# Two Gaussian blurs with a width per pixel: the exponents made on TensorE, the quotients turned on VectorE

## What is computed

```python
h = relu(einsum('bchw,co->bohw', x, w1) + b1[None, :, None, None])          # 32 hidden channels
ks = relu(einsum('bohw,o->bhw', h, w2[:, 0]) + b2[0]) * 20.0 + 1.0          # a width per pixel
sigma = ks / 3.0
logits = -gauss_kernel[None, None, None] / (2.0 * sigma[..., None, None] ** 2)
wgt = exp(logits)                                                            # 9 x 9 per pixel
wgt = wgt / sum(wgt, axis=(-2, -1), keepdims=True)
low_freq = sum over (u, v) of xp[:, :, u:u+64, v:v+64] * wgt[..., u, v]      # xp: x padded by 4
enhanced = x + low_freq
out = (enhanced - mean) / sqrt(var + 1e-5)                                   # over the plane
```

## Time and profile before

| | us |
|---|---|
| median of three runs | 515.1 |
| the three runs | 514.4, 515.1, 520.95 |
| span of the profiled execution, first to last instruction | 516.5 |
| TensorE busy in it | 431.7 (84%) |
| VectorE busy | 374.6 (73%) |
| ScalarE busy | 279.2 (54%) |
| GpSimd busy | 57.2 (11%) |

### The profile page before, as it was taken

One profiled execution on the slowest core, in us unless ns is written; L12 is line 12 of the kernel. 1 busy time (PEld: TensorE's weight loads), 2 busy tenths in 40 slices (PEclk: granted clock), 3 DMA queues, 4 the chain that ended last, 5 costly groups with the idle time before them and its releaser, 6 DMA issues. The chain is left out here.

```text
span 516.5 us, 16761 instructions
## 1 busy us (share of the span) xinstructions
PE 431.7 (84%) x7248; PEld 311.4 (60%) x7248; DVE 374.6 (73%) x563; ACT 279.2 (54%) x382; POOL 57.2 (11%) x76
## 2 busy tenths in 40 slices
PE   4578998877999649689999998469978899999971
PEld 2277952224988512357777787357746687777860
DVE  2695486763888875488999999239525899999953
ACT  0655476663333200189888888211015888888753
POOL 3230002321000000310000120000030000000000
PEclk9968999997999959999999999869987999999986
DMA  8840000000000000000000000000000000000004
GB/s 189 173 171 1 2 1 0 1 0 1 3 3 1 3 0 0 0 2 4 3 4 1 0 2 4 3 1 1 0 0 1 3 4 3 3 0 1 3 4 162
DMA packets 8088, 9.79 MB, mean 19 GB/s; under 512 B 5391, under 2 KB 6752, under 8 KB 7904
## 3 DMA queue, kind: packets, MB, share of 16 engines
q1 hardware_dynamic: 7008, 8.60, 6.0%
q10 hardware_dynamic: 1024, 0.36, 0.4%
HBM read 6.85 MB, written 2.11 MB: 17 GB/s over the span
## 5 line engine op out<-in xcount | busy, mean ns | idle before, releaser
L1110 DVE TENSOR_TENSOR g_wgt<-g_exponents,ps 128x1024 f32<-128x1024 f32 x128 | 150.9, 1206 | 4.4 <-PE ps L955 4.3
L1054 ACT ACTIVATE g_wgt<-g_wgt 128x1024 f32<-128x1024 f32 x128 | 132.4, 1061 | 18.6 <-DVE g_wgt L1110 17.7
L955 PE MATMUL ps<-ident,g_scl 128*128 128x128 f32 x512 | 78.9, 283 | 4.5 <-DVE g_scl L1101 3.6
L970 PE MATMUL ps<-g_wgt,g_xt 128*32 128x64 f32 x4096 | 72.6, 223 | 7.5 <-issue 7.4
L970 PEld LDWEIGHTS ps<-g_wgt,g_xt 128*32 128x32 f32 x4096 | 62.0, 111 | 27.2 <-issue 24.1
L955 PEld LDWEIGHTS ps<-ident,g_scl 128*128 128x128 f32 x512 | 56.3, 139 | 16.0 <-DVE g_scl L1101 4.7
L1038 ACT ACTIVATE g_hid<-ps,vec 128x512 f32<-128x512 f32 x32 | 22.0, 688 | 64.5 <-PE ps L914 64.5
L469 PE MATMUL ps<-conv_img,projblk 128*32 128x512 f32 x256 | 35.4, 673 | 0.0
L1351 PE MATMUL ps<-high,wb 128*128 128x512 f32 x72 | 30.6, 426 | 5.3 <-DVE rest L1380 5.3
L526 ACT ACTIVATE biased<-ps,beta_o 128x512 f32<-128x512 f32 x32 | 23.5, 746 | 13.6 <-PE ps L469 13.5
L1061 ACT COPY g_num<-ps 128x512 f32<-128x512 f32 x32 | 18.5, 578 | 22.0 <-PE ps L970 22.0
(11 more groups left out here) (163 smaller groups left out, 688.8 us busy)
## 6 DMA issues: line engine op xcount, KB each, us to landing
x<-in_x SPq DMA_DIRECT2D x8, 256.0 KB, 6.9
x<-in_x SPq DMA_DIRECT2D x1, 2048.0 KB, 8.2
out<-g_result SPq DMA_DIRECT2D x4, 512.0 KB, 3.9
windows<-band SPq DMA_DIRECT2D x4, 256.0 KB, 4.9
c_weight<-in_c_weight SPq DMA_DIRECT2D x1, 576.0 KB, 3.8
g_w<-in_g_w SPq DMA_DIRECT2D x2, 128.0 KB, 2.6
onehot<-in_onehot ACTq DMA_DIRECT2D x1, 128.0 KB
g_gband<-in_g_gband SPq DMA_DIRECT2D x2, 64.0 KB, 2.8
```

The source lines that it names most:

```text
L955: tr = pe.transpose(ps[:, u % 4, P * k:P * k + P], spread(scl[s][:, k, u:u + 1], [P, P]), ident[:])
L970: mm = pe.matmul(ps[32 * j:32 * j + 32, O_BANK, 64 * cb:64 * cb + 64], xt[(s + t) % 2][:, cb, b, :], wgt[s][b][:, t, cb, :], start=(t == 0 ...
L1054: act.activation(w, w, ACT.Exp).then_inc(weight, 1)
L1110: dve.tensor_tensor(wgt[s][u][:], spread(gband[:].unsqueeze(2), shape), spread(s_in, shape), ALU.mult).then_inc(logit, 1)
```

## The change

**Exponents.** The widths of a row no longer go through spreading and a product. GpSimd makes diagonal blocks (`pool_diag`): 32 x 32 matrices with the scale of a pixel on the diagonal, 16 of them side by side in 512 columns. TensorE multiplies the constant exponents, now stationary with pixels first, with these (`pe_fill`): four matmuls with K=32, one on each 32 partitions, into four PSUM banks. One call fills the exponents of two exponentials; a blur has 32 calls. ScalarE's exponential (`act_weight`) reads two banks of PSUM, 1,024 columns, and writes `wgt`. Three pairs of banks take turns.

**Quotients.** VectorE turns the numerators straight out of PSUM in blocks of 32 x 32 (`dve_swing`), divides (`dve_mix`) and turns the result back (`dve_low`); GpSimd adds it to the image (`pool_enhance`). TensorE and ScalarE have no part in this any more.

**Widths and turned image first.** The hidden layer of all eight rows stands at the start, its matmul as two with K=64, its relu half on ScalarE and half on VectorE; the scales come in two batches of four rows. All nine row groups of the image are turned before the fourth fill. The staged image lies in `wgt` buffers that aren't yet in use. The loop over rows is gone.

The core of the diff; the functions that it takes away are those printed above.

```diff
-        for name, shape in (("gmask", [P, 2, BLK * BLK]), ("outblk", [P, 2, 64]),
+        for name, shape in (("gmask", [P, 2, P]), ("outblk", [P, 2, 64]), ("hot", [P, 32]),
...
-    tile = [sb(f"tile{s}", [P, CB, BLK, QC]) for s in range(2)]
+    gband = sb("exponents", [P, 2, P])
+    hid = [[sb(f"hid{s}{i}", [P, CB, BLK, BLK]) for i in range(2)] for s in range(2)]
+    relu = sb("relu", [P, BANK])
+    sm = [sb(f"sm{i}", [P, 4 * 4 * B]) for i in range(2)]
+    scl = [sb(f"scl{i}", [P, 4, 4 * B]) for i in range(2)]
+    diag = [[sb(f"diag{s}{h}", [P, 16, 32]) for h in range(2)] for s in range(2)]
+    MX = C + 1
+    xt = [sb(f"xt{g}", [P, CB, B, MX]) for g in range(RB + 1)]
...
+    KS_BANK, XT_BANK, O_BANK = (4, 5), (6, 7), (6, 7)
+    BATCH = 4
+    XT_ON_ACT = 3
...
+        return 2 * (n % 3)
+    def pe_hidden(pe, r):
+        if r >= 2:
+            for i in range(2):
+                pe.wait_ge(hid_out[i], r - 1)
+        for i in range(2):
+            part = slice(64 * i, 64 * i + 64)
+            pe.matmul(ps[:, 2 * (r % 2) + i, :], w1[part, i, :],
+                      pad[part, BLK * r + R:BLK * r + R + BLK, R:R + W], start=True, stop=True).then_inc(hid_mm, 1)
...
+    def act_hidden(act, r):
+        act.wait_ge(hid_mm, 2 * r + 1)
+        if r >= 2:
+            act.wait_ge(ks_mm, r - 1)
+        act.activation(hid_to(r, 0), hid_in(r, 0), ACT.Relu, bias=vec[:, VEC[tag + "_b1"]:VEC[tag + "_b1"] + 1],
+                       scale=1.0).then_inc(hid_out[0], 1)
+    def dve_hidden(dve, r):
+        dve.wait_ge(hid_mm, 2 * r + 2)
+        if r >= 2:
+            dve.wait_ge(ks_mm, r - 1)
+        dve.tensor_scalar(hid_to(r, 1), hid_in(r, 1), vec[:, VEC[tag + "_b1"]:VEC[tag + "_b1"] + 1], 0.0,
+                          ALU.add, ALU.max).then_inc(hid_out[1], 1)
...
+    def tile(g):
+        spare = wgt[1][g // 4 % 2][:].rearrange("p t v u a n -> p (t v u a n)")
+        return spare[:, 1024 * (g % 4):1024 * (g % 4) + 1024].rearrange("p (k r c) -> p k r c", k=CB, r=BLK)
...
+    def pe_xt(pe, g):
+        pe.wait_ge(staged, 2 * g + 2)
+        for k in range(2):
+            if g > 0:
+                xt_evacuated(pe, g - 1, k)
+            for j in range(4):
+                cb = 4 * k + j
+                tr = pe.transpose(ps[:, XT_BANK[k], P * j:P * j + P],
+                                  tile(g)[:, cb].rearrange("p r c -> p (r c)"), ident[:])
+            tr.then_inc(xt_mm, 1)
+    def xt_copy(eng, copy, g, k, done):
+        eng.wait_ge(xt_mm, 2 * g + k + 1)
+        copy(xt[g][:, 4 * k:4 * k + 4, :, 0:C],
+             ps[:, XT_BANK[k], :].rearrange("p (k b m) -> p k b m", k=4, b=B)).then_inc(done, 1)
+    def pe_fill(pe, f):
+        r, h, t = f // 4, f // 2 % 2, f % 2
+        if t == 0:
+            pe.wait_ge(diag_ready, 2 * r + h + 1)
+        if f >= 1:
+            pe.wait_ge(weight, 2 * f - 1)
+        for g in range(4):
+            part = slice(32 * g, 32 * g + 32)
+            mm = pe.matmul(ps[:, pair(2 * f + g // 2) + g % 2, :], gband[part, t, :],
+                           diag[r % 2][h][part].rearrange("p a n -> p (a n)"), start=True, stop=True)
+        mm.then_inc(logit, 1)
+    def act_weight(act, n):
+        r, h, t, parity = n // 8, n // 4 % 2, n // 2 % 2, n % 2
+        act.wait_ge(logit, n // 2 + 1)
+        if r >= 2:
+            act.wait_ge(blurred, 2 * (r - 2) + h + 1)
+        act.activation(wgt[r % 2][h][:, t, parity].rearrange("p u a n -> p (u a n)"),
+                       ps[:, pair(n):pair(n) + 2, :].rearrange("p u n -> p (u n)"), ACT.Exp).then_inc(weight, 1)
+    def pe_blur(pe, r, h, parity):
+        pe.wait_ge(weight, 8 * r + 4 * h + 2 + parity + 1)
+        if parity == 0:
+            xt_evacuated(pe, RB if r == 0 else r + 1, 0)
+            xt_evacuated(pe, RB if r == 0 else r + 1, 1)
+            if r > 0:
+                pe.wait_ge(swung_out, 2 * (r - 1) + h + 1)
         for k in range(4):
...
+                for j in range(4):
+                    mm = pe.matmul(ps[32 * j:32 * j + MX, O_BANK[h], 64 * cb:64 * cb + 64],
+                                   xt[r + t][:, cb, 2 * j + h, :], wgt[r % 2][h][:, t, parity, :, 4 * k + j, :],
                                    start=(t == 0), stop=(t == 1))
+        if parity == 1:
             mm.then_inc(blurred, 1)
+    def dve_swing(dve, r, h):
+        dve.wait_ge(blurred, 2 * r + h + 1)
+        dve.transpose(swung[h][:].rearrange("p a n -> p (a n)"), ps[:, O_BANK[h], :]).then_inc(swung_out, 1)
+    def dve_mix(dve, r, h):
+        dve.wait_ge(swung_out, 2 * r + h + 1)
+        dve.reciprocal(rz[h][:], swung[h][:, :, C]).then_inc(rz_ready, 1)
+        dve.wait_ge(rz_ready, 2 * r + h + 1)
+        if r > 0:
+            dve.wait_ge(low_ready, r)
+        dve.tensor_tensor(mix[:, :, C * h:C * h + C], swung[h][:, :, 0:C], spread(rz[h][:].unsqueeze(2), [P, 16, C]),
+                          ALU.mult).then_inc(mixed, 1)
+    def dve_low(dve, r):
+        dve.wait_ge(mixed, 2 * r + 2)
+        if r >= 2:
+            dve.wait_ge(enhanced, r - 1)
+        dve.transpose(low[r % 2][:], mix[:].rearrange("p a n -> p (a n)")).then_inc(low_ready, 1)
+    def pool_enhance(pool, r):
+        pool.wait_ge(low_ready, r + 1)
+        rows = pixel_rows(r).rearrange("p r (k c) -> p r k c", c=BLK)
+        pool.tensor_tensor(rows, rows, low[r % 2][:].rearrange("p (k r c) -> p r k c", k=CB, r=BLK), ALU.add)\
+            .then_inc(enhanced, 1)
     def dve_stats(dve, r):
         dve.wait_ge(enhanced, r + 1)
...
+    def pool_diag(pool, r, h):
+        pool.wait_ge(small, 3 * (r // BATCH) + 3)
+        if r >= 2:
+            pool.wait_ge(logit, 4 * (r - 2) + 2 * h + 2)
+        own = scl[r // BATCH][:, r % BATCH].rearrange("p (a h) -> p h a", h=2)[:, h]
+        pool.tensor_tensor(diag[r % 2][h][:], spread(own.unsqueeze(2), [P, 16, 32]),
+                           spread(hot[:].unsqueeze(1), [P, 16, 32]), ALU.mult).then_inc(diag_ready, 1)
     def quarter(j):
         return (pad[:, R + 16 * j:R + 16 * j + 16, R:R + W],
                 result[:, j * PIX // 4:(j + 1) * PIX // 4].rearrange("p (h w) -> p h w", w=W))
...
         def _(pool):
+            pool.wait_ge(arrived[4], 16)
+            for g in range(RB):
+                pool_stage(pool, g)
+            for r in range(1):
+                for h in range(2):
+                    pool_diag(pool, r, h)
+            pool_stage(pool, RB)
+            for g in range(RB + 1):
+                pool.memset(xt[g][:, :, :, C:MX], 1.0).then_inc(ones_set, 1)
+            for r in range(1, 2):
+                for h in range(2):
+                    pool_diag(pool, r, h)
+            for r in range(RB):
+                if r + 2 < RB:
+                    for h in range(2):
+                        pool_diag(pool, r + 2, h)
+                pool_enhance(pool, r)
+                if r == 0 and to_clear is not None:
+                    pool.memset(to_clear[:], 0.0).then_inc(sem("cleared"), 1)
         @block.tensor
         def _(pe):
+            for a in arrived[:2]:
                 pe.wait_ge(a, 16)
+            pe_hidden(pe, 0)
+            for r in range(1, RB):
+                pe_hidden(pe, r)
+                pe_ks(pe, r - 1)
+                if r == BATCH + 1:
+                    pe_ks_turn(pe, 0)
+            pe_ks(pe, RB - 1)
+            pe_xt(pe, 0)
+            pe_ks_turn(pe, 1)
+            pe_xt(pe, 1)
+            pe_xt(pe, 2)
+            pe.wait_ge(band_ready, 1)
+            pe.wait_ge(small, 6)
+            for f in range(3):
+                pe_fill(pe, f)
+                pe_xt(pe, 3 + 2 * f)
+                pe_xt(pe, 4 + 2 * f)
+            pe.wait_ge(ones_set, RB + 1)
+            pe_blur(pe, 0, 0, 0)
+            pe_fill(pe, 3)
+            pe_blur(pe, 0, 0, 1)
+            for r in range(1, RB):
+                for q in range(4):
+                    pe_fill(pe, 4 * r + q)
+                    pe_blur(pe, r - 1 + q // 2, 1 - q // 2, q % 2)
+            for parity in range(2):
+                pe_blur(pe, RB - 1, 1, parity)
         @block.scalar
         def _(act):
+            for r in range(RB):
+                act_hidden(act, r)
+            for g in range(XT_ON_ACT):
+                xt_copy(act, act.copy, g, 0, xt_out_s)
...
         @block.vector
         def _(dve):
+            for a in arrived[2:4]:
                 dve.wait_ge(a, 16)
+            for r in range(BATCH):
+                dve_hidden(dve, r)
+                if r == 0:
+                    dve.scalar_tensor_tensor(out=gband[:].rearrange("p t m -> p (t m)"),
+                                             in0=gband_in[:].rearrange("p t m -> p (t m)"), scalar=-4.5,
+                                             in1=gmask[:].rearrange("p t m -> p (t m)"),
+                                             op0=ALU.mult, op1=ALU.add).then_inc(band_ready, 1)
+            dve_hidden(dve, BATCH)
+            dve_relu(dve, 0)
+            dve_hidden(dve, BATCH + 1)
+            dve_small(dve, 0)
```

(17 more changed lines are left out.)

367 lines of the change are left out of this document (78 added, 289 removed).

## The result

The changed kernel takes 484.0 us (median of four runs, 481.4 to 484.9), the kernel before 516.95 us (four runs, 514.4 to 520.95). The ratio is 0.937, with a 95% interval of 0.930 to 0.943. The forecast was 470 us with a range of 457 to 507: the sign and the mechanism hold, and the gain is 33 us where 45 were expected. The profiled execution took 483.4 us, with a span of 481.4 us (before: 516.5).

The account below looks back on a forecast made before the run. TensorE and VectorE were taken as nearly full in the blurs, with a TensorE-ScalarE loop as next bound. From 515.1 us, blur gains of 23.9 and 24.0 (47.9) were subtracted and 3 added for code: 470 us, range 457 to 507.

Parts of the forecast that it names:

- forecast case: Whole kernel: the summed forecast of 470 us holds, with a time of 458 to 482 us; chance 0.55.
- partial stops for code or further drains: Both blurs: a third to two thirds of the full code stalls, or extra tiling-change drains, 482 to 504 us; chance 0.18.
- The fill: Blurs: four K=32 matmuls on different partitions overlap and write exponents for two exponentials in 1.12 us.
- price in turn: Rival in the blurs: four K=32 tiles don't overlap, 3.7 us each time, 648 us total; in turn or pairs, chance 0.09.
- The loop: Steady blur rows: matmuls 1.12, exponential 1.04 and hops 0.09 us between TensorE and ScalarE make 2.25 us per round.
- TensorE's 2.09: Steady blur rows: TensorE's own time per round, 1.06 us for exponents plus 1.03 for a blur group, tiling changes included.
- a further drain: Blurs: an extra 0.13 us at each tiling change would make TensorE's round 2.35 us and the total some 6 us higher.
- The start: Each blur's beginning: hidden layer 13.6, then 4.4, 9.3 and 1.0 us, so the fourth exponent write comes 28.3 us in.
- The end: Each blur's last part, from its last exponent write through quotients, addition and statistics: 9.2 us.
- The second blur's 2 us: Second blur: slower clock at its start and ScalarE's table load keep it 2 us longer, 102.5 against 100.5 us.
- Code: Both blurs: fetching straight-line TensorE instructions costs 0 to 1.5 us per 256, 18 times; 1.5 us per blur was taken.
- The base: Whole kernel: gains are subtracted from 515.1 us, the median of the runs, 1.4 us below the profiled span of 516.5.

## Why the prediction was right, and where it was off

**Bound and sign.** Right. Both full engines lost work, and the next bound is the loop between TensorE and ScalarE, not an engine: half of the blur matmuls taken away leaves the rounds at 2.325 us, looser waits in the same work shorten them to 2.18. The 484.0 us themselves lie outside the forecast case (458 to 482 us, chance 0.55), in the band that the prediction had given to partial stops for code or further drains (482 to 504 us, 0.18). The traces show neither in that size; the time came there by the start and the hops, below.

**The fill.** Estimated 1.12 us, measured 1.14. Its price in turn, 3.7 us and 648 us in all, was right too (3.70, 645.1), but only with all rows at work; on one row tile the halved clock makes it 900.

**The loop.** Forecast 2.25 us, measured 2.325: 1.14 + 1.02 and 0.12 or 0.21 for the hops, where I had taken 0.09 from a round trip with a single wait in it. Fills that first wait for their diagonal as well start some 0.09 us later, although the diagonal lies ready; that the second wait is the reason was not tested. 28 x 0.075 = 2.1 us per blur. TensorE's 2.09 held as a sum; a further drain did not show.

**The start.** This term was mis-sized most. First fill at +18.8 us (forecast 18.0), fourth at +31.9 (28.3): 3.6 us per blur. The timeline of the changed kernel:

```profile
237.43 1.14 PE L1021 MATMUL ps<-g_diag,g_exponents 32*128 32x512 f32 x8
...
238.50 1.09 PE L1001 MATMUL ps<-ident,g_wgt 128*128 128x128 f32 x8
...
240.03 1.16 PE L1001 MATMUL ps<-ident,g_wgt 128*128 128x128 f32 x8 [0.44 <-DVE g_xt L1007]
...
241.12 1.14 PE L1021 MATMUL ps<-g_diag,g_exponents 32*128 32x512 f32 x8
...
245.82 1.09 PE L1044 MATMUL ps<-g_wgt,g_xt 128*17 128x64 f32 x64 [0.94 <-DVE g_xt L1007]
```

A step is 1.07 + 1.53 + 1.09 = 3.69 us, not 3.1. I compared sums (TensorE 3.0 us, VectorE 2.9 us) and took something above the larger. But two groups in a row go through the same two banks, and the round trip of a bank (transposes 0.5, copy 0.68, two hops) takes 1.53 us, longer than a group's 1.09 us. A group costs 1.09 us besides, not 0.98. The last step holds another 0.94 us, in which the first blur group waits for the last image copy; the prediction had no term for it. The remaining 0.8 us stand ahead of the first fill.

**The end.** 8.6 us against 9.2: the block transpose takes 0.72 us from the banks, where I had 1.1 from another layer's row, and GpSimd's addition 1.26, not 1.04. VectorE's work per row shrank with it, to 3.97 us where 5.4 were estimated. In the second blur the end takes 10.2 us, with a stop for code:

```profile
467.64 0.53 PE L1044 MATMUL ps<-g_wgt,g_xt 128*17 128x64 f32 x23 [1.33 <-issue]
```

**The second blur's 2 us.** I kept them for a slow clock and the table load. The clock was 1.00 and its table load lay beside other work. The blur is 1.9 us longer than the first all the same: 1.3 us is this stop, and 0.3 stands between its fourth and fifth fill (2.70 us instead of 2.38), where the blur group stops once more:

```profile
398.98 0.68 PE L1044 MATMUL ps<-g_wgt,g_xt 128*17 128x64 f32 x33 [0.39 <-issue]
```

So the size was right by luck, for a wrong reason.

**Code.** I had 1.5 us per blur; the trace has none in the first and 1.33 + 0.39 = 1.7 us in the second. The sum behind it was wrong too: a tenth of 18 stops of 1.5 us is 2.7 us per blur, and 1.5 us is one stop. With 2.7 the forecast would have been 472.6. Either was a guess between ends. What was missing is the pace: 256 instructions in 4.1 us pass with one stop of 0.39 us in the steady rounds of both blurs, in 3.85 us with rounds up to 0.3 us longer, and a demand for 256 in 2.9 us is held to 3.8. The stop of 1.33 us stands where three blur groups follow one another without a fill, 384 instructions; the same place in the first blur passed without a stop, in 3.2 us.

**Outside the blurs.** I gave the rest of the kernel no change; the first blur begins 3.1 us later. 1.3 us of this is one step that comes with the addresses. The rest differs from run to run (213.0 to 216.8 us in kernels with these addresses) and wasn't taken apart.

**The base.** I subtracted from 515.1, the median of three runs. Later medians of the same kernel are 516.5 to 520.0, and the changed kernel's profiled execution took 2.0 us more than its span. The account, from the forecast's 470.2 to 483.4 for the profiled execution: blurs 5.2 + 5.0, code not used -3.0, stage ahead 3.1, stage between -0.5, base 1.4 + 2.0, sum 13.2 us.

So the terms that were mis-sized are the sum for the start, twice 3.6 us, then the hops of the loop, twice 2.1. The unforeseen 3.1 us ahead of the first blur come next.

## What to carry to other kernels

Where two engines hand banks to each other, write down the loop (work, hop, work, hop) beside the busy sums; when the loop is the longest, wait for each buffer by itself instead of for the last of a set, which gave 8 us here without a change of work. The same holds for two groups in a row through the same banks: put other work between them. When code is unrolled, compare the new pace of instructions with the fastest that any trace has shown, since below that pace the supply cost next to nothing here, and above it it set the time.
